# Gathers of a message ring wait for the addition in place of the product (graph layer, mixer and routed experts)

## The chip, the cores and the metric

The kernel runs on one core of a Trainium2 chip. Its time is the device time of one execution in microseconds; where several runs are given, the number is their median.

## The reference, cut to what matters

A graph of 3125 nodes with 256 features and 53125 typed edges goes through one layer: a relational graph convolution in both directions, a linear attention mixer with an MLP, and a mixture of eight experts of which each token takes two. The change is in the graph convolution:

```python
def _typed_pass(feat, W, bias, src_idx, dst_idx, etypes, norm_per_edge, n):
    proj = jnp.einsum('ni,rio->rno', feat, W)        # 16 relations, 256 x 256 each
    m = proj[etypes, src_idx] + bias                 # one row of 256 per edge
    m = m * norm_per_edge[:, None]
    return segment_sum(m, dst_idx, num_segments=n)

xn = _layernorm(x)
m_forward  = _typed_pass(xn, Wf, ..., src, dst, etypes, norm_f, n)
m_backward = _typed_pass(xn, Wb, ..., dst, src, etypes, norm_b, n)
x = x + 2 * xn @ loop_weight + self_bias + m_forward + m_backward + mixer(xn)
x = x + experts(layernorm(x))
```

## The kernel before, in words

**Tables.** For each direction TensorE multiplies the 25 tiles of 128 nodes with the weights of all 16 relations (`project`, L674 to 681), 512 columns at a time. ScalarE copies each product out of its bank (`evacuate`, L667), and SyncE stores it to a table in HBM (`store_banks`, L685). A table has one row of 256 numbers per node and relation.

**Sorting.** VectorE and TensorE sort the edges by the tile of 128 nodes to which their sum goes. Each direction is cut into TE = 440 groups of 128 edges, and the edges of one group all go to the same node tile. Two directions make 880 groups, numbered n = 0 to 879 through the kernel.

**One group, four steps.** The work around the change is a pipeline over n, on four engines:

1. GpSimd gathers the 128 rows of the table that the edges need, 128 KB, with one indirect DMA (`gather`, L721 to 726). They land in place n % 16 of a ring of RING = 16 messages (`msg`, L712). The semaphore `s_ga[n % 16]` counts the landing.
2. VectorE makes the one-hot matrices that say which edge goes to which node of the tile, four groups at a time (`onehots`, L731 to 736), in a second ring of 16 places (`oh`). They are made behind the addition of every fourth group, for the groups 13 to 16 further on (L776).
3. TensorE multiplies the one-hot matrix with the message (`sum_tile`, L738 to 748, here called the product) into a bank of PSUM. It waits for the gather, for the one-hot matrices, and for the addition that last read the same bank (`user[n]`, L746). Sums take turns over three banks in the first part and four in the rest (`NARROW` and `SEG`, L716). The product counts the semaphore `s_sm` up by one.
4. VectorE adds the bank to the accumulator of the node tile (`add_sums`, L764 to 777, here called the addition). It waits for `s_sm`, and counts `s_ac` up by one. All additions are made in the order of n.

**Order of the work.** Each engine has one queue, written out by hand. GpSimd's holds little else in this part: it waits for the forward table and the sorted indices, issues gathers 0 to 439, waits for the backward table (L992 to 994), issues gathers 440 to 879, and after them waits for the end of the mixer. The products are spread evenly by hand between other work of TensorE (`forward_upto`, `rows_upto`, `keys_upto`, `attn_upto`, `mlp_step`, L781 to 807): forward products beside the projection of the backward direction, backward products beside the mixer (keys and queries L1777, key products L1805, attention L1844) and its MLP (L1867, L1876). VectorE's queue holds the additions in the same numbers beside its own part of that work, such as `loop_added` (L1210), the maximum over the keys (L1239) and the subtraction in `k_less` (L1249), which reads tiles that SyncE loads from mix_rows.

**The wait that the change touches.** A gather may overwrite place n % 16 only when the message of group n - 16 is no longer read. `G.wait` (L72) issues the wait only if its value is above zero, so the first 16 gathers have none:

```python
d, b = n // TE, n % RING
G.wait(s_sm, n - RING + 1)
e.indirect_dma_start(msg[b][:, 0:C], None, table[d], ...).then_inc(s_ga[b], 16)
```

The message is read by the product alone. The addition reads the bank that the product wrote, and waits for the product itself:

```python
e.wait_ge(s_sm, n + 1)
V.wait(s_ac, n)
to = acc[d][:, ds(column.pop(n), W)]
vec.tensor_tensor(to, to, ps[sum_bank(n)][:, 0:W], ALU.add).then_inc(s_ac, 1)
```

Of the kernel before, what the change touches and what calls it, by code (L numbers as in the profile page):

```python
# [101 lines left out]
def build(nc, a, out):  # L102
# [12 lines left out]
    with ctx:  # L115
# [7 lines left out]
        def sem(name, whole=False):  # L123

            nsem[0] += 1
            s_ = nc.alloc_semaphore(f"{name}_{nsem[0]}")
            if not whole:
                scope.append(s_)
            return s_
# [55 lines left out]
        G = Engine(None, nc.gpsimd, None)  # L185
# [103 lines left out]
        RING = 16  # L289
# [416 lines left out]
        def loop_xT(t):  # L706
# [11 lines left out]
        s_oh, s_sm, s_ac, s_ones, s_zf, s_zb = (sem(n) for n in  # L718
            ("onehots", "segment_mm", "accumulated", "ones_set", "zero_forward", "zero_backward"))

        def gather(e, n):  # L721

            d, b = n // TE, n % RING
            G.wait(s_sm, n - RING + 1)
            e.indirect_dma_start(msg[b][:, 0:C], None, table[d], bass.IndirectOffsetOnAxis(  # L725
                ap=idx[d][:, n % TE:n % TE + 1], axis=0)).then_inc(s_ga[b], 16)

# [251 lines left out]
        with nc.Block() as block:  # L979
            @block.gpsimd  # L980
            def _(e):
# [8 lines left out]
                for n in range(TE):  # L990
                    gather(e, n)
# [3 lines left out]
                for n in range(TE, 2 * TE):  # L995
                    gather(e, n)
# [1014 lines left out]
```

## Time and profile before

| what | value |
|---|---|
| time, median of 3 runs | 2249.82 us (2246.55 to 2253.24) |
| the profiled execution, time | 2245.63 us |
| the profiled execution, span of the core | 2243.7 us |
| TensorE matmul busy | 2015.8 us, 90% of the span |
| VectorE busy | 1138.3 us, 51% |
| GpSimd busy | 1027.6 us, 46% |
| ScalarE busy | 605.0 us, 27% |
| mean granted TensorE clock, share of full speed | 0.960 |

How to read it: busy time is summed per engine over the whole span, and engines work beside each other. A share says nothing by itself about what a shorter instruction is worth; for that one needs the chain of waits that ended last, and who waited for whom. Gathers run from 420.7 us to 1731.1 us of the span. What lies before is the forward table, and what lies behind is the routed experts. In the rows, PE is TensorE, PEld its weight loads, DVE VectorE, ACT ScalarE, POOL GpSimd and SP SyncE. A 32-bit product of 128 x 128 by 128 x 257 stands as two matmul records, so matmul counts of L748 are halved to count products.

### The profile page before, as it was taken

Reading aid. Unit: us, or ns where it says so; the run is one execution under the profiler, and the core shown is the slowest. Engines: PE = TensorE matmul, PEld = TensorE weight load, DVE = VectorE, ACT = ScalarE, POOL = GpSimd, SP = SyncE. Lnnn points to the kernel's source line nnn. Section 1 sums busy time; section 2 is a strip of 40 time slices with the busy share of each in tenths; the row PEclk is TensorE's granted clock in tenths of the full one; section 3 lists DMA queues with packets and bytes.
Section 4 is the critical chain, followed back from the end, with each engine's and each line's share of the span. In section 5 each row is a group of like instructions: output and inputs, shape, how many; then the busy total and the mean of one; then the engine's idle time right before and its main releaser. Section 6 shows DMA issues by size and latency. Waiting matters only on the chain.

```text
span 2243.7 us, 26429 instructions
## 1 busy us (share of the span) xinstructions
PE 2015.8 (90%) x8235; PEld 1379.3 (61%) x8235; DVE 1138.3 (51%) x2452; ACT 605.0 (27%) x1262; POOL 1027.6 (46%) x1014
## 2 busy tenths in 40 slices
PE   7999999889999999898878788898989669999997
PEld 3456544355555555454545555677777668888897
DVE  4999950256666564433566656544455841111121
ACT  2333333211221221111422221222222552222242
POOL 0000000366666666666566666666665113333332
PEclk9999999999999999999899999999999579999999
DMA  7432335455555555556644444332334384444473
GB/s 276 158 136 95 134 155 229 159 158 177 179 178 179 178 168 182 178 181 165 184 144 138 146 138 122 90 90 87 87 90 80 128 288 112 125 116 120 128 194 67
DMA packets 136486, 333.20 MB, mean 149 GB/s; under 512 B 25344, under 2 KB 65952, under 8 KB 135072
## 3 DMA queue, kind: packets, MB, share of 16 engines
q1 hardware_dynamic: 80064, 199.64, 24.5%
q0 software_dynamic: 52992, 130.09, 23.1%
q10 hardware_dynamic: 3296, 1.80, 0.3%
q8 instruction: 71, 1.16, 0.2%
q14 instruction: 63, 0.52, 0.1%
HBM read 202.71 MB, written 128.71 MB: 148 GB/s over the span
## 4 chain that ended last, share of the span: by engine, by line
PE 80%; issue 6%; another core or an unknown queue 5%; DVE 4%; ACT 3%; DMA 2%; DVEq 0%; POOL 0%; SPq 0%; ACTq 0%; POOLq 0%
PE bank L679 29%; PE bank L748 15%; PE bank L1947 9%; PE bank L1958 8%; PE bank L1867 4%; PE bank L1876 4%; PE bank L586 3%; DVE arena L773 1%; PE bank L1777 1%; PE bank L1805 1%; DMA table_fwd<-arena 1%; PE bank L1765 1%; PE bank L1844 1%; PE bank L1916 1%
## 5 line engine op out<-in xcount | busy, mean ns | idle before, releaser
L679 PE MATMUL bank<-arena,work 128*128 128x512 f32 x1600 | 741.9, 600 | 14.2 <-ACT arena L672 9.0
L773 DVE TENSOR_TENSOR arena<-arena,bank 128x257 f32 x880 | 370.8, 421 | 529.7 <-PE bank L748 284.1
L748 PE MATMUL bank<-arena 128*128 128x257 f32 x1760 | 499.2, 396 | 71.1 <-DVE arena L773 37.6
L725 POOL DMA_INDIRECT arena<-table_bwd,arena x440 | 428.3, 974 | 237.4 <-issue 99.0
L725 POOL DMA_INDIRECT arena<-table_fwd,arena x440 | 437.2, 994 | 212.8 <-issue 99.8
L679 PEld LDWEIGHTS bank<-arena,work 128*128 128x128 f32 x1600 | 301.3, 192 | 296.5 <-issue 270.8
L672 ACT ACTIVATE arena<-bank 128x512 f32<-128x512 f32 x400 | 238.5, 598 | 777.4 <-PE bank L679 551.7
L748 PEld LDWEIGHTS bank<-arena 128*128 128x128 f32 x1760 | 327.7, 197 | 194.8 <-issue 153.7
L1017 POOL DMA_INDIRECT out<-xn,work x56 | 89.4, 1597 | 250.9 <-DVE xn L192 181.3
L1947 PE MATMUL bank<-xn,arena 128*128 128x256 f32 (+1 forms) x1120 | 203.0, 340 | 0.0
L734 DVE TENSOR_TENSOR arena<-cst,arena 128x512 f32<-128x512 f32 x220 | 151.2, 689 | 102.0 <-PE bank L679 102.0
L1958 PE MATMUL bank<-arena 128*128 x896 | 199.0, 379 | 0.0
L1691 ACT ACTIVATE arena<-bank,work 128x256 f32<-128x256 f32 (+1 forms) x280 | 120.6, 431 | 286.7 <-PE bank L1947 278.5
L1947 PEld LDWEIGHTS bank<-xn,arena 128*128 128x128 f32 x1120 | 178.9, 192 | 17.0
L1486 DVE TENSOR_TENSOR xn<-bank,work 128x256 f32<-128x256 f32 x56 | 23.8, 425 | 321.5 <-PE bank L1958 321.5
L1958 PEld LDWEIGHTS bank<-arena 128*128 128x128 f32 x896 | 169.2, 190 | 22.4
L984 POOL MEMSET arena<- 128x6425 f32 x1 | 5.5, 5453 | 313.5 <-DVE gmap_bwd L193 313.5
L1867 PE MATMUL bank<-arena 128*128 128x256 f32 (+1 forms) x416 | 111.2, 390 | 25.7 <-ACT arena L1642 14.8
L1876 PE MATMUL bank<-arena 128*128 128x256 f32 x400 | 106.4, 388 | 8.0 <-ACT arena L1642 6.2
L1867 PEld LDWEIGHTS bank<-arena 128*128 128x128 f32 x416 | 79.2, 198 | 45.7 <-ACT arena L1642 19.4
L586 PEld LDWEIGHTS bank<-arena,work 128*128 128x128 f16 x832 | 67.2, 97 | 51.1 <-issue 46.5
L508 DVE TENSOR_TENSOR arena<-arena 128x648 f16<-128x648 f16 (+1 forms) x156 | 92.4, 607 | 8.8 <-PE bank L586 7.1
(315 smaller groups left out, 1563.8 us busy)
## 6 DMA issues: line engine op xcount, KB each, us to landing
table_fwd<-arena SPq DMA_DIRECT2D x100, 512.0 KB
table_bwd<-arena SPq DMA_DIRECT2D x100, 512.0 KB
arena<-in_W SPq DMA_DIRECT2D x35, 1024.0 KB
arena<-in_W SPq DMA_DIRECT2D x2, 4096.0 KB, 14.3
arena<-table_fwd,arena POOLq DMA_INDIRECT x440
arena<-table_bwd,arena POOLq DMA_INDIRECT x440
work<-x_transposed SPq DMA_DIRECT2D x50, 128.0 KB
mix_rows<-arena SPq DMA_DIRECT2D x25, 256.0 KB
```

Source lines behind the costliest of these rows:

```text
L586: last = pe.matmul(ps[bank][:, 0:2 * LT].rearrange("p (v l) -> p v l", v=2), ohv[:, c // QB, :, c % QB], abv[:, :, c // QB, :, c % QB], st ...
L672: act.activation(ar(STG0 + s % 8 * 512, 512), ps[4 + s % 2][:, :], ACT.Copy).then_inc(s_po, 1)
L679: last = pe.matmul(ps[4 + s % 2][:, :], xT[t % 2][:, k * P:(k + 1) * P], ar(W_off[d] + k * 4096 + c * 512, 512), start=(k == 0), stop=(k = ...
L725: e.indirect_dma_start(msg[b][:, 0:C], None, table[d], bass.IndirectOffsetOnAxis(ap=idx[d][:, n % TE:n % TE + 1], axis=0)).then_inc(s_ga[b ...
L734: vec.tensor_tensor(oh_all[:, b:b + 4, :], iota.unsqueeze(1).broadcast_to(four), loc[n // TE][:, c:c + 4].unsqueeze(2).broadcast_to(four), ...
L748: pe.matmul(ps[sum_bank(n)][:, 0:W], oh[b], msg[b], start=True, stop=True).then_inc(s_sm, 1)
L773: vec.tensor_tensor(to, to, ps[sum_bank(n)][:, 0:W], ALU.add).then_inc(s_ac, 1)
L1691: act.activation(hT7[u % 2][:, j * C:j * C + n], ps[1 + j % 4][:, 0:n], ACT.Gelu, bias=aux[u % AR][:, 4 + j:5 + j]).then_inc(s_c7, 1)
L1867: last = pe.matmul(ps[4 + j % 2][:, 0:n], ar(W1T_off + k * HID + j * P, P), z2T[:, k * C:k * C + n], start=(k == 0), stop=(k == 1))
L1876: pe.matmul(bank, hT[:, j * C + u * P:j * C + (u + 1) * P], ar(W2T_off + j * C, C), start=(j == 0), stop=False)
L1947: last = pe.matmul(ps[1 + j % 4][:, 0:n], w1b[u % 4][:, k * HID + j * P:k * HID + (j + 1) * P], xT7[u % 2][:, k * C:k * C + n], start=(k = ...
L1958: last = pe.matmul(ps[5 + t % 2][:, 0:C], h, arena[:, ds(x * 2048 + (WE2 + j * C), C)], start=(j == 0), stop=(j == 7))
```

## The change

One line of `gather` is changed. The gather into place n % 16 waits for the semaphore `s_ac`, which counts additions, in place of `s_sm`, which counts products. The value is the same, n - 15. Since an addition waits for its own product, the new wait includes the old one. No instruction is added or removed, and no buffer is moved.

```diff
         def gather(e, n):
 
             d, b = n // TE, n % RING
-            G.wait(s_sm, n - RING + 1)
+            G.wait(s_ac, n - RING + 1)
             e.indirect_dma_start(msg[b][:, 0:C], None, table[d], bass.IndirectOffsetOnAxis(
                 ap=idx[d][:, n % TE:n % TE + 1], axis=0)).then_inc(s_ga[b], 16)
```

## Rows read from the trace of the kernel before

**Rows 1.** The chain that ended last, share of the span by engine.
```profile
PE 80%; issue 6%; another core or an unknown queue 5%; DVE 4%; ACT 3%; DMA 2%; DVEq 0%; POOL 0%; SPq 0%; ACTq 0%; POOLq 0%
```

**Rows 2.** Costliest groups: line engine op, shapes xcount | busy us, mean ns | idle before.
```profile
L773 DVE TENSOR_TENSOR arena<-arena,bank 128x257 f32 x880 | 370.8, 421 | 529.7 <-PE bank L748 284.1
L748 PE MATMUL bank<-arena 128*128 128x257 f32 x1760 | 499.2, 396 | 71.1 <-DVE arena L773 37.6
L725 POOL DMA_INDIRECT arena<-table_bwd,arena x440 | 428.3, 974 | 237.4 <-issue 99.0
...
L734 DVE TENSOR_TENSOR arena<-cst,arena 128x512 f32<-128x512 f32 x220 | 151.2, 689 | 102.0 <-PE bank L679 102.0
```

**Rows 3.** Who waited for whom: us in total, times, longest us.
```profile
POOL arena L725 <- issue: 198.8, 624, 1.9
POOL arena L725 <- PE bank L748: 160.5, 207, 2.4
...
PE bank L748 <- DVE arena L773: 37.6, 24, 6.8
...
DVE arena L1249 <- DMA arena<-mix_rows: 20.5, 21, 2.0
```

**Rows 4.** Line L725: duration ns min/median/max; then who waited for it (us, times).
```profile
L725 POOL DMA_INDIRECT arena<-table_fwd,arena x440: 940/946/1496, 420.7 to 1065.4; - x147
...
  PEld bank L748: 3.7, 1
```

**Rows 5.** Instructions in order of time around 420 us: start us, us, engine.
```profile
420.70 1.14 POOL L725 DMA_INDIRECT arena<-table_fwd,arena  x1 [4.36 <-DMA table_fwd<-arena]
...
424.89 0.73 PEld L748 LDWEIGHTS bank<-arena 128*128 128x128 f32 x4 [3.67 <-DMA arena<-table_fwd,arena]
```

**Rows 6.** Stretches, line L725 alone: from:to length, POOL busy (xcount), clock, DMA.
```profile
400.00:700.00 300.00, 192.42 (x190) 0.97 0.54 171
...
400.00:1254.50 854.50, 557.60 (x563) 0.97 0.56 170
...
400.00:1500.00 1100.00, 715.10 (x725) 0.96 0.52 158
```

**Rows 7.** Stretches, line L748 alone: from:to length, PE busy (xcount), PEld busy (xcount).
```profile
400.00:700.00 300.00, 96.34 (x353) 63.15 (x354) 0.97 0.54 171
...
400.00:1254.50 854.50, 302.39 (x1102) 203.71 (x1102) 0.97 0.56 170
...
400.00:1277.00 877.00, 310.71 (x1125) 209.38 (x1126) 0.96 0.55 169
...
400.00:1500.00 1100.00, 397.91 (x1420) 264.07 (x1420) 0.96 0.52 158
```

**Rows 8.** DMA issues: line engine op xcount, KB each, median us to landing.
```profile
out<-X SPq DMA_DIRECT2D x1, 128.0 KB, 6.6
```

**Rows 9.** Instructions in order of time, 1253 to 1260 us, engines VectorE and GpSimd.
```profile
1253.06 0.42 DVE L773 TENSOR_TENSOR arena<-arena,bank 128x257 f32 x1 [0.21 <-DVE arena L773]
...
1254.55 0.95 POOL L725 DMA_INDIRECT arena<-table_bwd,arena  x1 [0.31 <-issue]
1255.80 0.95 POOL L725 DMA_INDIRECT arena<-table_bwd,arena  x1 [0.30 <-issue]
...
1258.50 0.94 POOL L725 DMA_INDIRECT arena<-table_bwd,arena  x1 [0.30 <-issue]
...
1259.33 0.42 DVE L773 TENSOR_TENSOR arena<-arena,bank 128x257 f32 x1
```

**Rows 10.** Stretches, line L773 alone: from:to length, DVE busy (xcount), clock, DMA.
```profile
400.00:1254.50 854.50, 230.38 (x547) 0.97 0.56 170
```

**Rows 11.** TensorE in order of time, around 1278 us.
```profile
1278.41 0.60 PE L748 MATMUL bank<-arena 128*128 128x257 f32 x2
```

**Rows 12.** GpSimd in order of time, the last two gathers.
```profile
1729.86 0.95 POOL L725 DMA_INDIRECT arena<-table_bwd,arena  x1 [0.30 <-issue]
1731.11 0.94 POOL L725 DMA_INDIRECT arena<-table_bwd,arena  x1 [0.30 <-issue]
```

**Rows 13.** TensorE in order of time, the last two products (two records each).
```profile
1744.38 1.03 PE L748 MATMUL bank<-arena 128*128 128x257 f32 x4
```

## The prediction

> **What bounds the kernel now.** I read the chain of waits first. TensorE holds 80% of it and GpSimd, which issues the gathers, holds 0% [rows 1]. So a gather costs time only where TensorE stands and waits for its rows. The groups by cost come next: 440 gathers per direction, mean 974 ns in the second one, 1760 matmul records of the product at L748 (two for each of the 880 products), and 880 additions at L773 of 421 ns [rows 2]. The list of waits says what GpSimd waits for: in 207 cases a product, 160.5 us together, and in 624 cases nothing but its own 0.32 us between instructions (198.8 / 624). TensorE waited for additions 24 times, 37.6 us [rows 3]. The view of L725 turns this round and asks who waited for a gather: TensorE's weight load did once, 3.7 us, and no row there names a second case [rows 4]. That one is the first product of all: gather 0 starts at 420.70 and its product at 424.89 [rows 5].
>
> What matters is therefore the lead, that is how many gathers have been issued whose product has not started. The count of each line up to one time gives it. At 700 us 190 gathers and 353 / 2 = 176.5 products have started, a lead of 13.5. At 1254.5 us it is 563 against 1102 / 2 = 551, or 12. At 1500 us it is 725 against 710, or 15 [rows 6, 7]. From 700 to 1500 us 535 gathers were issued in 800 us, so one product is due every 1.50 us. A lead of 12 to 15 is 18 to 22.5 us. What a gather needs, from its start to the start of the product that reads it, is 424.89 - 420.70 = 4.2 us [rows 5]. That the landing alone takes longer elsewhere is possible: the slowest transfer of 128 KB for which the page has a landing takes 6.6 us [rows 8]. With the longer issue of that first gather, 1.14 us, I take 7.7 us as the upper bound of the need.
>
> **The change, part by part.** It removes no instruction and adds none. Each gather n from 16 on keeps one wait on a constant; only the counter differs. Before, it waited until product n - 16 had read its place. Now it waits until addition n - 16 has been made, which comes after that product. So no gather can start earlier by this edit, and some start later. How much later?
>
> *Ordinary case.* Where GpSimd stood at a product, it now stands one addition longer: 0.42 us [rows 2], and some 0.2 us for the signal to be seen, the idle time that the trace shows between a wait and the next addition [rows 9]. That is 0.6 us. It doesn't add up from gather to gather, because an unhindered gather takes 1.25 us from start to start (1254.55 to the next ones, four of them up to 1258.50 with one short wait [rows 9]) while one is due only every 1.50 us: 0.25 us is made good per gather. The path that sets the end gets 0, because a lead of 18 us less 0.6 stays over 7.7.
>
> *Long pauses of additions.* VectorE is sometimes late with them. The clearest place is 1253.06 to 1259.33, with no addition begun in between [rows 9]. At 1254.5 us 547 additions had started, numbers 0 to 546 [rows 10], and 563 gathers, numbers 0 to 562. Gather 563 started at 1254.55. Under the new wait it needs addition 547, the one that begins at 1259.33 and ends at 1259.75. So gather 563 moves to about 1260.0, 5.5 us later, and the three behind it, up to 1258.50, move with it at 1.25 us each. When is their message due? Up to 1277 us 1125 / 2 = 562.5 products have started, so product 563 is the one at 1278.41 [rows 7, 11]. Its lead was 23.9 us and will be 18.4, against 4.2 to 7.7 needed. Nothing is late. The next on GpSimd's queue are only more gathers; its lag is made good after 5.5 / 0.25 = 22 gathers, or 33 us. The store and load queues of SyncE, and the one-hot matrices, wait for nothing that GpSimd does here.
>
> *The end of the list.* No further product hides the last gathers. Gather 878 and 879 are the rows at 1729.86 and 1731.11; the last product is the second pair in the group at 1744.38, about 1744.8 [rows 12, 13]. The lead is 13.7 us, and 13.1 us with 0.6 us of delay. It exceeds 7.7 us by 5.4. The list's first 16 gathers have no wait in either kernel, so the one wait of TensorE, 3.7 us, stays as it is.
>
> *What the trace doesn't show* is whether gathers that start elsewhere in time disturb other work. Below: VectorE waited 20.5 us for the loads of mix_rows [rows 3], just in the stretch where gathers move most; all of it could go at best, -20.5 us. Above: these 21 waits could double, +20.5 us. A gather moves 128 KB whenever it runs, and the number of them per us is the same, so I take 0, the value nearest to every row above.
>
> **Sum:** 0 us + 0 us + 0 us. The profiled execution took 2245.63 us (span 2243.7 and 1.9 around it) and stands 0.19% under the median of the three runs, 2249.82. I forecast the median unchanged, **2249.8 us**.
>
> **Rivals.**
> *Slower: the lead runs out behind pauses.* Held places shorten the ring from 16 to 16 less the additions outstanding, which the banks limit to three or four. If the remaining lead falls below 7.7 us at a product, TensorE waits. That takes a delay above 5.4 us in a place with a lead like that of the end, 13 us. Delays of 5.5 us exist [rows 9], but there the lead was 23.9. With one gather time of 0.97 us lost in each of the 24 places where TensorE met a late addition, the loss is 23 us, 2273 us. Chance 0.05.
>
> *Slower: GpSimd becomes the bound.* It would, if a gather with its 0.30 us took over 1.50 us on average; now it is 0.97 + 0.32 = 1.29. Gathers now start right behind an addition, where every fourth time the one-hot comparison of 689 ns begins [rows 2]. Lengthened by all of it, one in four takes 1.94 us, and the mean is (3 x 1.25 + 1.94) / 4 = 1.42 us, still under 1.50. Only if all took the longest of before, 1496 ns [rows 4], would it be 880 x (1.80 - 1.50) = 264 us more, 2514 us. Chance 0.01.
> The Trainium skill, SBUF — State Buffer, section "Who interferes with whom", says that a VectorE instruction with two SBUF inputs takes a shared read port from a GpSimd instruction that reads SBUF, and that the later of the two stands still; the comparison has two such inputs, and it speaks against this change. The spread of gathers from 940 to 1496 ns [rows 4] allows such a thing, but the sum above stays at 0 even with every fourth gather hit.
>
> *Faster: transfers meet less.* Half of the 20.5 us above would be 10 us, 2240 us. For it speaks that the delayed gathers lie in that stretch; against it, that the amount moved per us is unchanged. Chance 0.05.
>
> *The edit has no bite.* The counter of additions rises by one per addition in order, so the wait does what it says; where additions keep up it is already met. This gives 2249.8 as well and is in the forecast's chance.
>
> **Numbers.** Forecast 0.87, the two slower rivals 0.06, an unforeseen small loss 0.02, faster 0.05. A measurement of this kernel can tell about 0.3%, 6.7 us, from no change; the runs before span 2246.55 to 2253.24. The range is the forecast with that 6.7 us, taken a little further above, since a held gather can only start later: 2243 to 2258 us. Both ends of the unknown cost (20.5 us) lie outside it, with the 1 in 10 that it leaves out.
>
> **What the profile after would show.** Right: GpSimd's idle time named by the addition L773 in place of the product L748; its gathers 530 to 600 ns later there; a lead at 700 and 1500 us lower by under one; the gather number 563 near 1260 us; TensorE's wait for a gather still one case near 425 us. Wrong: TensorE or its weight load waiting for gathers several times, the mean gather above 1.2 us, or 20 us less in the waits for mix_rows.

## The result: 1.6% slower, and the profile after

The changed kernel takes **2285.53 us** (median of 4 runs, 2280.52 to 2287.96) against 2249.09 us of the kernel before in the same comparison (4 runs, 2246.55 to 2253.24). The ratio is **1.016, 95% interval 1.0142 to 1.0178**. Its profiled execution took 2283.28 us with a span of 2281.4 us, 37.7 us more than the span before.

The page first: the busy line, the chain of waits by engine, and the groups that answer to [rows 1, 2].

```profile
PE 2030.4 (89%) x8235; PEld 1387.2 (61%) x8235; DVE 1138.1 (50%) x2452; ACT 607.3 (27%) x1262; POOL 1037.1 (45%) x1014
...
PE 75%; DVE 7%; another core or an unknown queue 7%; issue 6%; ACT 2%; DMA 2%; DVEq 1%; SPq 0%; POOL 0%; ACTq 0%; POOLq 0%
...
L773 DVE TENSOR_TENSOR arena<-arena,bank 128x257 f32 x880 | 370.6, 421 | 556.9 <-PE bank L748 280.1
L748 PE MATMUL bank<-arena 128*128 128x257 f32 x1760 | 505.7, 399 | 102.8 <-DVE arena L773 83.2
L725 POOL DMA_INDIRECT arena<-table_bwd,arena x440 | 433.5, 985 | 258.4 <-DVE arena L773 131.0
```

No work became dearer: the addition still takes 421 ns, the gather 985 ns in place of 974, TensorE is busy 14.6 us longer. Over the span TensorE is idle 23.1 us longer (251.0 against 227.9 us) and busy 14.6 us longer, which together make the 37.7 us. GpSimd still holds 0% of the chain. So the chain got longer mostly by waiting, and not by waiting for gathers. The other shares are less firm: TensorE holds 75% where it held 80%, and "another core or an unknown queue" 7% where it was 5%, but in a second profile of the changed kernel (r_after) they are 79% and 6%. The list of waits (us in total, times, longest us) shows the same; it answers to [rows 3].

```profile
POOL arena L725 <- issue: 234.5, 647, 2.0
POOL arena L725 <- DVE arena L773: 233.9, 231, 4.4
...
PEld bank L748 <- issue: 192.2, 319, 10.6
...
DVE arena L773 <- remote: 154.8, 63, 10.7
...
PE bank L748 <- DVE arena L773: 83.2, 46, 9.9
...
DVE arena L1249 <- DMA arena<-mix_rows: 20.4, 20, 2.0
```

GpSimd stands at the ring about as long as before. Before it was 160.5 us at products [rows 3] and 78.2 us at a releaser called "remote" (its row is shown in the next section), together 238.7 us in 254 cases. Now it is 233.9 us in 231 cases, all named by the addition. What grew is elsewhere. TensorE waits for additions 83.2 us in place of 37.6, VectorE waits 154.8 us for "remote" in place of 112.9, and the weight load before a product waits 192.2 us with nothing that names its releaser, in place of 153.7.

The instructions of L725 by table (ns min/median/max, first and last start), and who waited for them, answer to [rows 4].

```profile
L725 POOL DMA_INDIRECT arena<-table_fwd,arena x440: 941/949/1467, 418.2 to 1080.9; - x147
L725 POOL DMA_INDIRECT arena<-table_bwd,arena x440: 942/949/1463, 1094.2 to 1772.9; - x147
...
  PEld bank L748: 3.7, 1
  PE bank L748: 2.9, 1
```

The forward gathers reach over 1080.9 - 418.2 = 662.7 us where they took 1065.4 - 420.7 = 644.7; the backward ones over 678.7 us where the same view of the kernel before (next section) gives 656.5. What lies before the first gather and behind the last product is as long as it was within 3 us. So all of the loss lies in the stretch with gathers and products. The two rows in which TensorE waited for a gather, once for its weight load and once for its matmul, hold 6.6 us; the kernel before has the same two with 3.7 and 2.8 us (next section).

Now the lead, by the counts of both lines up to 700, 1283.5 and 1500 us. First L725 alone, then L748 alone, in the columns of [rows 6, 7].

```profile
400.00:700.00 300.00, 188.52 (x186) 0.97 0.53 167
...
400.00:1283.50 883.50, 560.61 (x563) 0.95 0.54 164
...
400.00:1500.00 1100.00, 694.60 (x699) 0.94 0.51 154
```

```profile
400.00:700.00 300.00, 96.41 (x346) 61.21 (x346) 0.97 0.53 167
...
400.00:1283.50 883.50, 307.77 (x1103) 204.22 (x1104) 0.95 0.54 164
...
400.00:1500.00 1100.00, 390.45 (x1372) 255.52 (x1372) 0.94 0.51 154
```

At 700 us it is 186 - 173 = 13, at 1283.5 us 563 - 551.5 = 11.5, at 1500 us 699 - 686 = 13. It was 13.5, 12 and 15. The ring stays full, as forecast. The last gather and the last products answer to [rows 12, 13]: they are at 1772.89 and about 1783.5 us, a lead of 10.6 us (13.7 before), and TensorE waits for no gather there.

```profile
1772.89 0.94 POOL L725 DMA_INDIRECT arena<-table_bwd,arena  x1 [0.30 <-issue]
...
1783.08 1.03 PE L748 MATMUL bank<-arena 128*128 128x257 f32 x4
```

### The profile page after: what moved, and what is told of

It is laid out like the page before. It is cut to its first block, busy times and chain, and to the rows that moved or that the text cites. A ratio compares the mean times of both kernels' runs of the same rounds, so it can differ in the third digit from the quotient of the medians.

```text
span 2281.4 us, 26429 instructions
## 1 busy us (share of the span) xinstructions
PE 2030.4 (89%) x8235; PEld 1387.2 (61%) x8235; DVE 1138.1 (50%) x2452; ACT 607.3 (27%) x1262; POOL 1037.1 (45%) x1014
## 3 DMA queue, kind: packets, MB, share of 16 engines
q0 software_dynamic: 52992, 130.09, 23.1%
## 4 chain that ended last, share of the span: by engine, by line
PE 75%; DVE 7%; another core or an unknown queue 7%; issue 6%; ACT 2%; DMA 2%; DVEq 1%; SPq 0%; POOL 0%; ACTq 0%; POOLq 0%
PE bank L679 27%; PE bank L748 14%; PE bank L1947 9%; PE bank L1958 8%; PE bank L1867 4%; PE bank L1876 4%; DVE arena L773 3%; PE bank L586 2%; PE bank L1805 1%; DMA table_fwd<-arena 1%; PE bank L1844 1%; PE bank L1916 1%; PE bank L1926 1%; PE bank L1936 1%
## 5 line engine op out<-in xcount | busy, mean ns | idle before, releaser
L773 DVE TENSOR_TENSOR arena<-arena,bank 128x257 f32 x880 | 370.6, 421 | 556.9 <-PE bank L748 280.1
L748 PE MATMUL bank<-arena 128*128 128x257 f32 x1760 | 505.7, 399 | 102.8 <-DVE arena L773 83.2
L725 POOL DMA_INDIRECT arena<-table_bwd,arena x440 | 433.5, 985 | 258.4 <-DVE arena L773 131.0
L725 POOL DMA_INDIRECT arena<-table_fwd,arena x440 | 441.4, 1003 | 226.8 <-issue 119.3
L748 PEld LDWEIGHTS bank<-arena 128*128 128x128 f32 x1760 | 327.8, 197 | 232.3 <-issue 192.2
```

The source lines that it names most:

```text
L748: pe.matmul(ps[sum_bank(n)][:, 0:W], oh[b], msg[b], start=True, stop=True).then_inc(s_sm, 1)
```

## What a lost microsecond looks like: counts of products that arrive late

A long stall of the changed kernel stands between 971 and 981 us. Instructions in order of time, by engine: VectorE, TensorE, ScalarE, GpSimd (start, length, engine, line, in brackets the idle time before and what ended it).

```profile
971.70 0.42 DVE L773 TENSOR_TENSOR arena<-arena,bank 128x257 f32 x1 [1.00 <-issue]
978.79 0.42 DVE L773 TENSOR_TENSOR arena<-arena,bank 128x257 f32 x1 [6.66 <-remote]
...
971.95 1.03 PE L748 MATMUL bank<-arena 128*128 128x257 f32 x4
...
974.53 1.03 PE L748 MATMUL bank<-arena 128*128 128x257 f32 x4
979.36 1.08 PE L748 MATMUL bank<-arena 128*128 128x257 f32 x2 [3.80 <-DVE arena L773]
...
976.64 0.60 ACT L672 ACTIVATE arena<-bank 128x512 f32<-128x512 f32 x1 [6.48 <-remote]
...
979.48 0.94 POOL L725 DMA_INDIRECT arena<-table_fwd,arena  x1 [3.23 <-DVE arena L773]
```

Two products are recorded from 971.95 to 972.98 us and two from 974.53 to 975.56. The addition that needs the first of them starts at 978.79, some 6 us after that product should be over by its record. Its line waits only for that product's count and for the addition before it, which is long done. ScalarE, which waits for the projection's count, stands 6.48 us too. So "remote", which in a program of one core can't be another core, is here a count of TensorE that comes late. By the semaphores' numbers in the packed traces of the kernels before and after, every "remote" wait is at a semaphore that TensorE raises. TensorE then finds no free bank, waits 3.80 us for the addition, and GpSimd is held behind the same addition for 3.23 us.

The Trainium skill, Perfetto Trace Analysis, section "Tensor Engine Instruction (MATMUL, LD_WEIGHTS)", says that the end of a TensorE instruction in the profile is estimated from its size and not observed. That fits: the record ends and the count comes 6 us later.

The packed trace also keeps the moments at which semaphores were raised; no view prints them, so these are my reading of it. TensorE's records from 971.5 to 975.6 us lead to six counts, in this order: projection, two products, projection, two products. They were raised at 976.55, 978.66, 978.70, 978.76, 978.80 and 978.85 us. Four matmuls of the projection, which start 0.43 us apart by their records, stand between the third count and the fourth, and these two counts are 0.06 us apart. So that work was done before, and its count was held back. For the first two of the six it stays open whether the work or the count was late. VectorE and ScalarE started within 0.13 us of the counts. The counts were raised late, and not seen late.

One caution on all rows of waits: in the gather stretch the trace of the kernel before keeps 1098 of the 1453 moments at which TensorE raised a count and 941 of VectorE's 1693. A wait put down to "issue" there can be one whose releaser is missing.

The kernel before has such stalls too. Its instructions around 450 us, which I had not read before the forecast:

```profile
448.00 0.60 PE L748 MATMUL bank<-arena 128*128 128x257 f32 x2
...
453.31 0.60 ACT L672 ACTIVATE arena<-bank 128x512 f32<-128x512 f32 x1 [12.17 <-remote]
...
454.88 0.42 DVE L773 TENSOR_TENSOR arena<-arena,bank 128x257 f32 x1 [7.83 <-remote]
```

And the rows of its list of waits, and of its view of L725, that the forecast passed over:

```profile
PEld bank L748 <- issue: 153.7, 303, 7.2
...
DVE arena L773 <- remote: 112.9, 49, 7.8
...
POOL arena L725 <- remote: 78.2, 47, 3.8
```

```profile
L725 POOL DMA_INDIRECT arena<-table_bwd,arena x440: 940/946/1412, 1074.6 to 1731.1; - x147
...
  PE bank L748: 2.8, 1
```

Up to 420 us, with TensorE and ScalarE at the same projection but no gathers and no products, the list of waits of the kernel before has no row with "remote", and behind 1750 us, after the last product, it has none either. The stalls belong to the stretch in which gathers, products and additions run together. At VectorE's additions the changed kernel has more of them: 49 cases with 112.9 us become 63 with 154.8.

## The experiments

All change the wait at L724 alone, except where said. The ratio is that to the kernel before in the same comparison. The ratios are those on record, and a quotient of two medians can differ from them by up to 0.15%. There were five comparisons. The record numbers their chips 14, 4, 3, 8 and again 3, and the kernel before took 2231.21, 2250.14, 2230.45, 2246.57 and, in the last one, 2078.6 us. "Held" is a gather that GpSimd could have issued earlier.

| run | gather n waits for | median us | ratio, 95% interval |
|---|---|---|---|
| a_prod1 | product n-15 | 2235.37 | 1.001 (0.9997 to 1.0024) |
| b_prod2 | product n-14 | 2232.81 | 1.0006 (0.9993 to 1.0019) |
| r_prod2 | the same again | 2232.06 | 1.0004 (0.9995 to 1.0014) |
| h_prod4 | product n-12 | 2229.95 | 1.0001 (0.9987 to 1.0015) |
| c_both_old | product n-16, then addition n-20 | 2236.25 | 1.0022 (1.0011 to 1.0034) |
| i_prod4_ac | product n-12, then addition n-16 | 2235.59 | 1.0022 (1.0008 to 1.0036) |
| d_fwd_only | addition n-16 forward, product n-16 backward | 2246.44 | 1.0053 (1.0033 to 1.0073) |
| r_after | the change again: addition n-16 | 2284.47 | 1.0162 (1.0134 to 1.0189) |
| r2_after | the change again | 2267.31 | 1.0168 (1.0149 to 1.0187) |
| e_ac_plus1 | addition n-15 | 2281.42 | 1.0151 (1.0123 to 1.0178) |
| f_ac_prod2 | addition n-16, then product n-14 | 2278.88 | 1.0128 (1.0099 to 1.0156) |
| g_ac_prod4 | addition n-16, then product n-12 | 2280.08 | 1.0148 (1.0119 to 1.0178) |
| j0_mirror_only | product n-16; second count kept by VectorE | 2245.77 | 1.0002 (0.999 to 1.0015) |
| j1_pool_on_mirror | that second count of additions, n-16 | 2295.02 | 1.0216 (1.0196 to 1.0237) |
| k_ac_four | addition n-13, every fourth gather only | 2315.01 | 1.0297 (1.0268 to 1.0326) |
| l_oh | the one-hot matrices of group n | 2356.82 | 1.0504 (1.0459 to 1.0549) |
| m_sm_ahead | product n-16, in an instruction ahead of the gather | 2079.98 | 1.0005 (0.9993 to 1.0016) |
| n_sm_own | product n-16, carried by the gather | 2080.09 | 1.0003 (0.9994 to 1.0013) |

### First: is it the lead, the watched counter, or each direction's share?

**a_prod1** and **b_prod2** hold the gather for one and two products more, so they take the lead away and leave the counter.

```diff
-            G.wait(s_sm, n - RING + 1)
+            G.wait(s_sm, n - RING + 2)     # a_prod1; + 3 in b_prod2
```

> Gather n waits for product n - 15 in place of n - 16: held one product (about 1.5 us) longer, without the additions' count. Theory LEAD (a later gather costs by itself): its hold is over twice the 0.6 us that the change adds, so at least the loss of the change, over +36 us against before. Theory COUNTER (GpSimd waiting on the count of additions is what costs): 0 within 7 us. Theory PAUSE (gathers held behind late additions come in bursts after them and disturb the pairing of TensorE and VectorE): 0 to +20 us, as a product comes earlier than its addition in a pause.

> Gather n waits for product n - 14: held two products (about 3 us) longer. LEAD: more than the kernel above, about twice it, +70 us. COUNTER: 0 within 7 us. PAUSE: within 20 us of before, near the kernel above.

Measured 1.001 and 1.0006: nothing. A gather that starts one or two products later costs nothing, so the loss isn't the lead.

**c_both_old** keeps the old wait and adds one on additions, which is met already when it is reached.

```diff
             G.wait(s_sm, n - RING + 1)
+            G.wait(s_ac, n - RING - 3)
```

> Gather n waits for product n - 16 as before, and also for addition n - 20, which is nearly always long made. So GpSimd watches the count of additions, but no gather is held by it. COUNTER: the whole loss, about +36 us. LEAD and PAUSE: 0 within 7 us; one more instruction in GpSimd's queue per gather is hidden under the 0.25 us that each gather has to spare.

Measured 1.0022, interval 1.0011 to 1.0034: a real but small loss, a seventh of the change's. Looking at the counter of additions, with one more instruction per gather, is not what costs 1.6%.

**d_fwd_only** makes the change for gathers 0 to 439 alone.

```diff
-            G.wait(s_sm, n - RING + 1)
+            G.wait(s_ac if n < TE else s_sm, n - RING + 1)
```

> The changed wait for the 440 forward gathers alone; the backward ones wait for products as before. From the two profiles the stretch up to the 440th addition lost about 21 us and the rest about 18. If the loss is made locally: +18 to +23 us. If it depends on what the kernel does beside it in one half only: 0 or +36 us.

Measured 1.0053, a third of the loss; by the medians it is 15.2 us, less than the 18 to 23 us expected of a loss made locally. In its view of L725 the forward gathers reach over 655.5 us and the backward ones over 653.5. The three kernels above, on the same chip, have 641.0 to 645.7 and 650.3 to 657.4 us: the loss stays in the direction that has the new wait. It was no mishap at one place of the schedule.

### Second: a later addition, and product waits on top of the new one

**r_after** repeats the change on another chip. **e_ac_plus1** holds for one addition more. **f_ac_prod2** and **g_ac_prod4** add a product wait to the change, so that the gather is mostly released by a product again.

```diff
-            G.wait(s_sm, n - RING + 1)
+            G.wait(s_ac, n - RING + 1)     # r_after, r2_after
+            G.wait(s_ac, n - RING + 2)     # e_ac_plus1, alone
+            G.wait(s_ac, n - RING + 1)     # f_ac_prod2 and g_ac_prod4,
+            G.wait(s_sm, n - RING + 3)     # with + 5 in g_ac_prod4
```

> The changed kernel once more, on the chip of this comparison, so that its loss stands beside the kernels below. All theories: +1.2 to +1.8%, 27 to 40 us over before.

> Gather n waits for addition n - 15 in place of n - 16: still released by an addition, one later. PHASE (what costs is that a gather begins right behind an addition, together with what else that addition releases): the loss of the changed kernel, +30 to +40 us, not more. PAUSE (what costs is that gathers are held back while additions are late, and lead is lost there): clearly more than the changed kernel, +45 us or over.

> Gather n waits for addition n - 16 and for product n - 14. Product n - 14 mostly ends after addition n - 16, so that most gathers are released by a product, and only in pauses of the additions by an addition. PHASE: most of the loss gone, under +12 us. PAUSE: the loss of the changed kernel stays, +30 us or over.

> Gather n waits for addition n - 16 and for product n - 12, which with three or four banks cannot begin before addition n - 15 or n - 16. The wait for the addition is then never the last. PHASE: 0 within 10 us. PAUSE: gathers are held in pauses all the same, since the products wait for the additions there: +30 us or over. LEAD, weakened by the kernels before: a hold of four products, 6 us, is over the margin of 5.4 us that the prediction worked out, +10 us or over at the places with the least lead.

The change repeats: 1.0162. One addition more costs no more, 1.0151, so the loss does not grow with how long the gather is held. The two with product waits on top still lose 1.0128 and 1.0148, which I had not expected of g_ac_prod4: its strictest wait is on a product. Its list of waits shows why it need not be harmless:

```profile
POOL arena L726 <- DVE arena L774: 200.4, 215, 4.9
...
DVE arena L774 <- remote: 143.6, 63, 6.1
...
POOL arena L726 <- PE bank L749: 73.4, 99, 11.4
...
PE bank L749 <- DVE arena L774: 50.4, 39, 5.4
```

215 of its held gathers are still put down to an addition. The first wait in the source is carried by the gather itself and a second one stands in an instruction of its own ahead of it. Here the product wait is that second one. A held gather begins behind an addition once more, as these rows show (VectorE, then GpSimd):

```profile
973.76 0.42 DVE L774 TENSOR_TENSOR arena<-arena,bank 128x257 f32 x1 [2.42 <-PE bank L749]
...
974.37 0.94 POOL L726 DMA_INDIRECT arena<-table_fwd,arena  x1 [1.90 <-DVE arena L774]
```

The addition ends at 974.18 and the gather begins 0.19 us later. But this addition does not release it. Product n-12 waits for its bank, and so for addition n-15 or n-16; when its count comes, the addition that the gather asks for is already made. The profile names the addition because it is the last event near the start. So in g_ac_prod4 the last wait is TensorE's, and only the count that the gather itself carries is VectorE's.

### Third: the same waits in the other order

**r2_after** and **r_prod2** repeat a loser and a harmless one on a third chip. **h_prod4** waits for product n-12 alone, and **i_prod4_ac** has the waits of g_ac_prod4 with their places exchanged.

```diff
-            G.wait(s_sm, n - RING + 1)
+            G.wait(s_sm, n - RING + 5)     # h_prod4, and first in i_prod4_ac
+            G.wait(s_ac, n - RING + 1)     # i_prod4_ac only
```

> The changed kernel, so that it stands on one chip with the three kernels below: +1.2 to +1.8% if chips agree; the comparison that held the product kernels was on a chip where the kernel before is 19 us faster, and there it might be less.

> Product n - 14 alone, again: within 0.3% of before, if the earlier result is not the chip's.

> Gather n waits for product n - 12 alone. If the loss of the kernel with product n - 12 and addition n - 16 came from the long hold (LEAD), then the same here, +1.2 to +1.6%. If it came from the wait for the additions (WAITING ON THE COUNT), within 0.3% of before.

> Product n - 12 first and addition n - 16 second: the same two waits as before in the other order, so that GpSimd never stands at the count of additions, it only finds it reached. LEAD: as the kernel with product n - 12 alone plus nothing. WAITING ON THE COUNT (GpSimd standing at the very count that TensorE and VectorE wait for is what costs): the loss is gone, under 0.4%. If it still loses over 1%, while product n - 12 alone loses nothing, then naming that count in GpSimd's queue is enough, however seldom it stands there.

Holding the ring four products back costs 0.0% (h_prod4). That settles the lead: from a gather's start to that of its product the median is 14.2 us here and 20.1 in the kernel before (my count of the traces). That is 6 us off the lead, ten times the 0.6 us by which the change moves a gather. And i_prod4_ac, with the conditions of g_ac_prod4 and only their places exchanged, costs 0.22% in place of 1.48%. The waits of h_prod4 and, from the view in order of time, one of its held gathers (VectorE, then GpSimd):

```profile
POOL arena L725 <- PE bank L748: 158.6, 188, 10.4
...
DVE arena L773 <- remote: 106.1, 48, 4.8
...
POOL arena L725 <- remote: 70.3, 47, 2.8
```

```profile
791.57 0.42 DVE L773 TENSOR_TENSOR arena<-arena,bank 128x257 f32 x1 [2.50 <-remote]
...
791.70 0.94 POOL L725 DMA_INDIRECT arena<-table_fwd,arena  x1 [1.42 <-remote]
```

One count of TensorE releases both engines: the addition starts at 791.57 and the gather at 791.70, beside it and not behind it. VectorE's wait for "remote" is 106.1 us in 48 cases, as in the kernel before (112.9 in 49), and in the changed kernel on the same chip it was 139.3 in 58.

### Fourth: is it the shared counter? And fewer, larger waits on VectorE

In the change GpSimd watches the counter on which VectorE itself waits before each addition. **j0_mirror_only** lets VectorE raise a second count `s_gc`, which nobody reads; **j1_pool_on_mirror** lets the gathers wait for that one, so that nobody but GpSimd watches it.

```diff
 def add_sums
-                e.wait_ge(s_sm, n + 1)
                 V.wait(s_ac, n)
+                if n > 0:
+                    e.sem_inc(s_gc, 1)
+                e.wait_ge(s_sm, n + 1)
 def gather
-            G.wait(s_sm, n - RING + 1)
+            G.wait(s_gc, n - RING + 1)     # j1_pool_on_mirror only
```

> VectorE, which waits before each addition for the one before it, now also raises a second count there, one short instruction per addition, and makes that wait ahead of the one for the product. Gathers wait for products as in the kernel before; nobody reads the second count. This prices the second count alone: within 0.5% of before.

> Gathers wait for that second count, which says of the additions the same as the first, a little later (at VectorE's next turn). Theory SHARED COUNT (GpSimd standing at the count at which TensorE stands costs): as the kernel with the second count alone, within 0.4%. Theory VECTORE'S COUNT (standing at any count that VectorE raises costs), or the hold by additions as such: +1.2 to +1.8% over it.

The second count alone costs 1.0002, nothing. The gathers on it cost 1.0216, more than the change. So the shared counter is not the cause. The waits of j0_mirror_only first, then those of j1_pool_on_mirror, where the count is raised by VectorE's queue (DVEq):

```profile
DVE arena L776 <- remote: 138.6, 65, 11.4
...
PE bank L749 <- DVE arena L776: 29.5, 14, 8.0
```

```profile
POOL arena L726 <- DVEq L773: 237.7, 210, 5.5
...
DVE arena L776 <- remote: 155.1, 70, 9.0
```

VectorE waits for late counts 138.6 us in j0_mirror_only, which loses nothing, about as long as in r2_after (139.3), which loses 1.68%. So more of these waits do not by themselves mean a longer run.

**k_ac_four** waits for additions at every fourth gather only. **l_oh** waits, at every gather, for the one-hot matrices of its own group, which VectorE makes once in four additions and right behind one.

```diff
-            G.wait(s_sm, n - RING + 1)
+            if n % 4 == 0:
+                G.wait(s_ac, n - RING + 4)     # k_ac_four
+            if n >= RING:
+                G.wait(s_oh, n // 4 + 1)       # l_oh
```

> Only every fourth gather waits, for the addition n - 13, which covers the three behind it. The count is the shared one, but GpSimd stands at it a quarter as often, if longer each time. If the loss goes with the number of times: +0.3 to +0.6%. If it goes with the time that GpSimd stands there, or with being released by additions: +1.2 to +1.8%.

> Gathers wait for the count of one-hot matrices, which VectorE raises behind every fourth addition (the one of n - 13 or before), and at which TensorE stands only for every fourth product. SHARED COUNT: at most a quarter of the loss, under 0.6%. VECTORE'S COUNT or release by VectorE's work: +1.2 to +1.8%.

A quarter of the waits costs 2.97%, nearly twice the change; l_oh costs 5.04%. Both are far above what any of the theories named, 1.8% at most. The loss is not proportional to the number of waits. Both let gathers out in bunches of four behind VectorE: k_ac_four holds 92 gathers for 250.7 us, an average of 2.7 us, in place of 231 for 233.9.

```profile
POOL arena L726 <- DVE arena L774: 250.7, 92, 6.3
...
DVE arena L774 <- remote: 179.5, 67, 12.1
```

### Fifth: the moment of the gather, or who raises the count

In every loser the held gathers begin for the most part just behind VectorE's work (by my count of the traces 0.27 us behind the end of an addition in the change, 0.18 in f_ac_prod2 and g_ac_prod4), and in all but those two the count that releases them is always one that VectorE raises. In g_ac_prod4 it is TensorE's and in f_ac_prod2 it can be either, but in both the gather itself carries the wait for VectorE's. **m_sm_ahead** was to tell the two apart with TensorE's count alone. It puts the product wait into an instruction ahead of the gather, which in g_ac_prod4 made gathers begin some 0.5 us later, that is behind the addition. **n_sm_own** has the same two waits with the places exchanged. `s_ones` is counted once, long before.

```diff
-            G.wait(s_sm, n - RING + 1)
+            G.wait(s_ones, 1)                  # m_sm_ahead
+            G.wait(s_sm, n - RING + 1)         # exchanged in n_sm_own
```

> The gather waits for product n - 16 as in the kernel before, but in an instruction of its own ahead of the gather, and the gather's own wait is for a count of GpSimd's that has long been reached. In the profile of the kernel with product n - 12 and addition n - 16 that made a held gather begin some 0.75 us behind the product in place of 0.27 us, that is right behind an addition. PHASE (it costs to begin a gather 0.75 us or more behind the count of a product): +1.2 to +1.8%. VECTORE'S COUNT (only waits on counts that VectorE raises cost): as the next kernel, within 0.4%.

> The same two waits, the other way round: the gather itself waits for product n - 16, the instruction ahead of it for the count that has long been reached. A held gather then begins 0.27 us behind the product. Both theories: within 0.4% of before (one more instruction in GpSimd's queue, as in the earlier kernel at +0.22%).

Measured 1.0005 and 1.0003, no difference. But they don't decide it, since this comparison ran where the kernel before takes 2078.6 us, 7% to 8% less than in the other four. The list of waits of n_sm_own there has no row with "remote" at all:

```profile
POOL arena L726 <- PE bank L749: 93.9, 253, 8.8
...
PEld bank L749 <- issue: 62.5, 240, 2.8
...
PEld bank L749 <- DMA arena<-table_bwd,arena: 29.6, 39, 1.9
```

GpSimd waits for products 93.9 us in 253 cases, 0.37 us each. That is hardly over its 0.30 us between two instructions; by my count of both traces only 12 and 17 gathers followed an idle time of GpSimd above 0.45 us. Gathers of the forward table go from 418.0 to 993.3 us, 575.3 us in place of 644.7, at 1.31 us per gather, hardly over the 1.25 of an unhindered one. Among the backward ones the gathers are often the pace: TensorE's weight load waits for 39 of them. With almost nothing held, the place of the wait can't matter. In this comparison, without late counts, the same kernel ends 152 to 172 us earlier (2230.45 and 2250.14 less 2078.6). How much of that the late counts cost is not shown.

## Why the prediction was wrong

Forecast 2249.8 us, range 2243 to 2258; measured 2285.53. Point by point.

**What bounds the kernel.** Right as far as it went: TensorE bounds, GpSimd's own time is free, the ring is full. But the chain of [rows 1] also gave 5% to "another core or an unknown queue" in a program of one core, and 6% to "issue". That is some 250 us that I did not follow. The 5% are late counts: each of these waits in the chain ends at a semaphore of TensorE. The 6% stayed, and can hide releasers that the trace did not keep. Two readings of the rows were off as well, without weight for the result: the view of L725 does name a second wait for the first gather (2.8 us, the matmul's own, shown above), and the view behind [rows 8] has a landing of 6.9 us for 128 KB, so that the bound is 8.0 and not 7.7 us.

**Ordinary case, the later start.** A held gather now waits 233.9 / 231 = 1.01 us on average where it was 238.7 / 254 = 0.94 us. By my count of the traces a gather begins at the earliest 0.27 us behind the recorded end of product n - 16 before and 0.84 us after: 0.57 us later, where I forecast 0.6. The size of the delay was right. The step that failed stands right behind it: "The path that sets the end gets 0, because a lead of 18 us less 0.6 stays over 7.7." The lead did stay (13, 11.5 and 13 messages), and h_prod4 shows that even 6 us off it cost nothing. The conclusion was wrong, because a gather acts on the path in another way than by its rows being late.

**Long pauses.** Pauses of additions exist (978.79 above), and the gathers behind them do come later. Gather 563, forecast near 1260 us, is the one at 1284.19, as the stretch up to there has slid by some 30 us (it started at 1254.55 before); no product waited for it. e_ac_plus1 and h_prod4 say that the length of the hold itself has no price.

**End of the list.** Lead 10.6 us where I forecast 13.1; nothing late. The bound of 7.7 us itself was too low for a gather: where a trace has landings, in n_sm_own, they come 2.6 to 11.7 us after the start, median 3.1.

**What the trace doesn't show.** This is the term of the sum to which the loss belongs: whether gathers that start at another moment disturb other work. I put it at 0 because as many gathers run per us as before, and 37.7 us were measured. I bounded an unseen effect by the waits for mix_rows, 20.5 us. Those are 20.4 us after the change, untouched. A better bound from the same view was the waits without a named releaser: "remote" at the addition, 112.9 us, and the weight load's 153.7 us of "issue", which rose by 41.9 and 38.5 us. TensorE's waits for additions rose by 45.6 us. These overlap and are not to be added, but each is of the size of the loss, 37.7 us.

**The rivals.** "Slower: the lead runs out behind pauses" gave 2273 us and came nearest, for a wrong reason: 24 waits for additions did become 46, yet TensorE waited for gathers only 6.6 us, and a_prod1, b_prod2 and h_prod4, which shorten the lead far more, lose nothing. "GpSimd becomes the bound" falls: a median gather takes 949 ns where it was 946, the mean of the backward ones is 985 where it was 974, and the maximum is 1467 ns where it was 1496. With that falls what the Trainium skill's page "SBUF — State Buffer" would have added; gathers behind an addition are hardly stretched. The same section infers that making DMA descriptors needs the write interface, which such a VectorE instruction leaves free, and the rows fit that. "The edit has no bite" falls, as does the faster rival.

**What was to be seen in the profile after.** The idle of GpSimd is named by the addition, as written. The lead at 700 us fell by 0.5, at 1500 us by 2, more than the "under one" written. The sign that I named for being wrong, TensorE waiting for gathers several times, did not come, and the time rose all the same.

**What is shown of the cause, and what isn't.** Shown: the loss lies in the gather stretch, in the direction that has the wait (d_fwd_only). It is neither the lead (a, b, h), nor the longer hold (e, h), nor the watching of the counter or a second wait (c and i at 0.22%), nor sharing it with VectorE (j1), nor the number of waits (k). What goes with the loss is that TensorE waits longer for banks: 46.2 to 83.2 us for additions in the kernels that lose in both directions, 26.9 to 42.0 us in those that lose nothing or next to nothing. Late counts at VectorE part them less clearly (j0_mirror_only). In the first four comparisons every kernel whose gathers follow a product loses 0.0 to 0.2%, and every one whose gathers follow VectorE's work in both directions loses 1.3% to 5.0%.

The comparison of g_ac_prod4 (1.48%) and i_prod4_ac (0.22%) speaks for the moment at which the gather begins, as their conditions are the same and only the start moves by some 0.5 us. Against it stands that the two never ran on one chip, though the change itself lost alike on both (1.0162 and 1.0168). A rival fits the same two runs, and every other one: in each kernel that loses, the gather itself carries the wait for a count that VectorE raises, and in each harmless one of the first four comparisons it carries one of TensorE's. That VectorE must be the last to release is ruled out by g_ac_prod4, where TensorE's product is last. Still open are whether it is the moment or the count that the gather carries, since m_sm_ahead ran where hardly anything is held, and why TensorE's counts come late at all. One guess, that held gathers and additions in step disturb TensorE's writes or counts, was not tested by any run. In the kernel before, 97 of 138 late counts come 1.6 us or more behind the start of the last gather, where only a tenth of the stretch lies; but its held gathers wait for the same counts, so this doesn't tell cause from effect.

**The clock took part.** The granted clock of TensorE is 2.4 GHz or half of it, so a mean below 1 is time at half speed. Over 1100 to 1400 us, L748 alone, before and then after:

```profile
1100.00:1400.00 300.00, 114.50 (x401) 76.04 (x402) 0.95 0.46 139
```

```profile
1100.00:1400.00 300.00, 111.75 (x382) 74.25 (x381) 0.89 0.46 137
```

0.89 for 0.95 in 300 us means (0.95 - 0.89) x 2 x 300 = 36 us more at half speed. By my count TensorE is at half speed for 150 us of the gather stretch in the changed kernel's first profile and for 96 us in the kernel before. Of the 28 falls in the changed kernel 18 follow soon upon a pause of TensorE above 1 us, as in the stall shown, and 10 follow none. The lower clock can directly explain at most the 14.6 us that TensorE is busy longer, not the 23.1 us that it is idle longer. Nor is it needed for the loss: the profiled execution of r2_after has 102 us at half speed, nearly as little as the kernel before, and at 2262.40 us it is still 1.4% slower than the 2230.45 beside it.

## What to carry to other kernels

A wait that is later by less than the slack is not free by that alone: in this kernel, letting the gathers wait on VectorE's counts in place of TensorE's cost 1.3% to 5.0%, where TensorE's counts came late at times, while holding it four products longer on TensorE's count cost nothing. So keep a ring's release on the product that last reads the place, and if it must be later, on a later product. And where a profile of one core gives chain time to "another core or an unknown queue" or to a waiting engine's "remote", follow those rows before costing an edit at zero; here VectorE's "remote" waits alone were 112.9 us, where the forecast had taken 20.5 us as the bound of what it couldn't see.

## What the hardware did that I had not expected

- Counts of TensorE are raised many microseconds after the recorded end of the matmul: some 6 us in the stall shown, and then five counts within 0.19 us, with four matmuls between two of them. The longest idle times put down to it are 7.8 us (VectorE) and 12.2 us (ScalarE) in the kernel before, 10.7 and 11.9 us after. In these traces it happens only in the stretch in which gathers and products run.
- The same kernel takes 2230 to 2250 us in four comparisons and 2078.6 us in the fifth (23 runs, 2072.29 to 2083.94), where no late count is in the trace, with more DMA traffic at once: 194 GB/s from 420 to 1060 us against 175. Heavy traffic alone therefore doesn't make the counts late. What differs between the two is not known; the third and the fifth comparison have the same chip number, 3, on record, so the chip alone doesn't explain it if that number names one chip.
- Which of two waits the DMA instruction carries itself decides when it starts: in g_ac_prod4 and i_prod4_ac the conditions are the same, and by my count of the traces a released gather begins at the earliest 0.75 us behind the recorded end of product n-12 in the first, and 0.27 us in the second.
